# Decoder layer with a mixture of experts: expert tiles begun from the lists of five blocks, inside the cross-attention stage

## The chip, the cores and the metric

The kernel runs on one core of a Trainium2 chip. The metric is device time in microseconds (us), a median over runs. Engines are named as in the profile: PE is TensorE, DVE is VectorE, ACT is ScalarE, POOL is GpSimd, SP is SyncE.

## What is computed

The input is `x`, 4 sequences of 1024 tokens with 256 channels, and a context of 77 rows for each sequence. Three sublayers follow one another; after each one comes a residual and a layer norm:

```
x = layernorm(x + attn(x))         # gated delta rule: q, k, v projections, 4-tap causal convolution, silu, l2norm
x = layernorm(x + xattn(x, ctx))   # 16 heads of 64 over 77 context rows, masked softmax
x = layernorm(x + ffn(x))          # 8 experts, the top 2 of each token

probs = softmax(x @ router_w.T); keep the top 2, divide by their sum
g = x @ gate_w[e] + gate_b[e];  u = x @ up_w[e] + up_b[e]        # 256 -> 512
y = sum over the two experts of probs[e] * ((silu(g) * u) @ down_w[e] + down_b[e])
```

## The kernel before

Tokens are handled in 32 tiles of 128, and 4 tiles form a block, so there are 8 blocks. There are five stages, each with its own `Block` of five instruction streams, one per engine; a stage begins when all streams of the one before have ended. Every stream is written out by hand, runs in its written order, and waits on semaphores. There is no scheduler.

**`project_stage`** (line 100). For each block PE turns the normalised input (L335), makes eight column tiles of q, k, v (L379) and four gate tiles (L391). ACT copies each product out of PSUM twice (L463, L467), DVE adds three taps of the convolution to it (L617, three per column tile), PE turns the result back (L371) and ACT applies silu into `tok` (L456). POOL squares q and k (L299, two instructions of 128x1024 per block, in `squares`), DVE sums the squares (L603), and POOL makes the norms (L309 to L313) and scales `tok` by them (L316).

**`delta_stage`** (line 674). The recurrence. Near its end POOL fills `blank`, which SP stores over the DRAM tensor `list`: weight 0, and as destination one spare row of `y`.

**`cross_stage`** (line 1614). For each tile `g` of 32 a chain runs over all engines: PE scores, DVE scales them out of PSUM (`scaled_out`, L2189), POOL adds the mask (L1780), DVE takes the maximum and subtracts it (L2197, L2199), ACT takes exp (L2001), DVE sums and inverts (L2205, L2207), POOL scales (L1786), PE turns the weights and multiplies by V and the output projection (`attended`, L1885). After block `n` comes its norm (`x2t`, L1792, L1794, L2233, L2021), the store to the DRAM tensor `x2` (L1721), and the routing, one or two blocks late: `x2_turned` (L1899), `logits` (L1909), softmax and `top_two` on DVE, `counts` (L1916, L1917), and `entries` (L2130 to L2146), which gives each pair of token and expert a place in its expert's region of `list`. POOL writes the entries with eight indirect DMAs for each block (`listed_rows`, L1771). Behind the last block, DVE's `tile_list` (L2151 to L2166) turns the counts into two rows of 71 numbers: for each expert tile its expert (`tile_e`) and its place in the list (`tile_r`). SP also loads the experts' weights in this stage: gate and up early, down and the biases after block 6 (L2306 to L2314), into memory that the cross stage has used until then.

**`expert_stage`** (line 2318). 71 tiles of 128 entries (64 full ones and 7 for remainders), each of one expert. For tile `j`: SP loads its entries (L2361), DVE casts the two row numbers (L2497), POOL gathers 128 rows of `x2` (L2371), PE turns them (L2404), ACT copies (L2459), PE makes gate and up (L2415), DVE adds the biases (L2505 twice), ACT takes silu (L2464), DVE multiplies (L2512), PE turns (L2425), ACT copies (L2470), PE multiplies by the down weights (L2436), DVE adds the bias (L2519) and then weight and residual (L2523; the residual row is kept by ACT, L2477). POOL scatters the 128 rows to `y` (L2380), the token's first expert into the lower half of `y`, the second into the upper half. The next scatter waits until the one before has landed. PE's order is: gate and up of `j`, turn of the rows of `j+1`, turn of hidden `j-1`, down of `j-2`.

```
for j in range(FT + 2):
    if j < FT:
        known[j] = expert(pe, j)
        gate_up(j, known[j])
    if j + 1 < FT:
        x_turned(j + 1)
    if 1 <= j <= FT:
        h_turned(j - 1)
    if j >= 2:
        down(j - 2, known.pop(j - 2))
```

**`final_stage`** (line 2543). SP loads both halves of `y` block by block (16 DMAs of 512 KB, L2570, four blocks in flight), DVE adds the halves (L2608) and takes the moments (L2611, L2614), ACT the deviation (L2592), DVE inverts it (L2601, L2603), ACT normalises (L2584, four per block) and issues the store (L2588).

## Time and profile before

| | |
|---|---|
| median of 3 runs | 1759.49 us (1757.08 to 1759.88) |
| the profiled execution | 1761.76 us, span 1760.0 us |
| busy: PE, DVE, ACT, POOL | 1522.7, 1123.7, 735.7, 664.8 us |
| mean granted TensorE clock | 0.933 |
| DMA | 177.17 MB, mean 101 GB/s |

The span is the time from the first to the last instruction of the profiled execution. Busy time is a union: a PE row "x4" with 1.88 us is four matmuls that are issued one after the other and overlap, so its length is not four times the mean of one. In a timeline row the bracket tells how long the engine stood idle before it, and on whom it waited. POOL's DMA rows are the time in which it makes the descriptors; the transfer comes after. Clock 1.00 is full speed (2.4 GHz), 0.50 is half (1.2 GHz).

### The profile page before, as it was taken

How to read it: one execution, taken by the hardware profiler on the slowest of the kernel's cores; microseconds unless marked ns; L12 is line 12 of the kernel's file. 1: busy time of each engine (PE TensorE's matmuls, PEld its weight loads, DVE VectorE, ACT ScalarE, POOL GpSimd, SP SyncE). 2: the span in 40 equal slices, each digit the busy share in tenths (PEclk: the TensorE clock that was granted, in tenths of full speed). 3: DMA queues.
4: the chain of work that ended last, by engine and by line, in shares of the span. 5: the costliest groups of instructions: out<-in, count | busy, mean ns of one | idle time of the engine just before them, and what ended most of it. 6: DMA issues, size and time to landing. Idle time of an engine off the chain costs nothing. (4 is left out here: it accounts for less than half of the span.)

```text
span 1760.0 us, 30667 instructions
## 1 busy us (share of the span) xinstructions
PE 1522.7 (87%) x10698; PEld 1080.1 (61%) x10698; DVE 1123.7 (64%) x2342; ACT 735.7 (42%) x1625; POOL 664.8 (38%) x539
## 2 busy tenths in 40 slices
PE   6999954799999999957999999997379999999970
PEld 3555523788888887624777677776246666666640
DVE  5999985577777864522558787777434555555445
ACT  4667641234434444624455554542023333333324
POOL 1475646212333311011436555656423333333320
PEclk9999975799999999969999999998589999999995
DMA  3233337645556543261023230006011111111118
GB/s 103 85 132 119 148 134 191 165 119 163 149 156 151 137 123 137 85 208 56 6 79 128 85 126 28 13 25 224 29 28 49 46 46 46 47 49 43 49 34 286
DMA packets 180126, 177.17 MB, mean 101 GB/s; under 512 B 79640, under 2 KB 138700, under 8 KB 179852
## 3 DMA queue, kind: packets, MB, share of 16 engines
q1 hardware_dynamic: 163963, 145.23, 27.1%
q0 software_dynamic: 10400, 22.95, 3.9%
q10 hardware_dynamic: 5616, 7.08, 1.2%
q8 instruction: 87, 1.43, 0.3%
q14 instruction: 60, 0.48, 0.1%
HBM read 115.39 MB, written 59.81 MB: 100 GB/s over the span
## 5 line engine op out<-in xcount | busy, mean ns | idle before, releaser
L617 DVE SCALAR_TENSOR_TENSOR conv_y<-conv_in,taps,conv_y 128x512 f32<-128x512 f32 x192 | 185.1, 977 | 11.7 <-ACT conv_y L467 7.0
L2380 POOL DMA_INDIRECT y<-o,idx x71 | 83.5, 1176 | 241.6 <-DVE o L2523 233.8
L2459 ACT ACTIVATE xsT<-pX 128x256 f32<-128x256 f32 x71 | 27.3, 384 | 303.4 <-PE pX L2404 303.4
L2415 PE MATMUL pG<-w_gu,xsT 128*128 x284 | 135.5, 600 | 1.2 <-issue 0.6
L1831 PE MATMUL xQ<-late,last 128*128 128x512 f32 x256 | 128.4, 625 | 8.9 <-ACT late L1987 4.8
L2415 PE MATMUL pU<-w_gu,xsT 128*128 x284 | 134.3, 595 | 0.0
L2436 PE MATMUL pD<-late,hT 128*128 x568 | 134.2, 379 | 0.0
L379 PE MATMUL ps_j<-xnT,w_qkv 128*128 128x512 f32 x256 | 122.6, 603 | 0.0
L1786 POOL TENSOR_TENSOR sc<-sc,den 128x1232 f32<-128x1232 f32 x32 | 72.0, 2251 | 109.2 <-DVE den L2207 109.0
L2436 PEld LDWEIGHTS pD<-late,hT 128*128 128x128 f32 x568 | 102.5, 190 | 11.0
L2519 DVE TENSOR_TENSOR o<-pD,late 128x256 f32<-128x256 f32 x71 | 30.2, 425 | 121.4 <-PE pD L2436 121.4
L991 POOL DMA_DIRECT2D x<-x1t x32 | 18.3, 572 | 223.2 <-ACT x1t L1337 223.2
L1780 POOL TENSOR_TENSOR sc<-sc,madd 128x1232 f32<-128x1232 f32 x32 | 82.7, 2585 | 37.6 <-DVE sc L2189 37.6
L2415 PEld LDWEIGHTS pU<-w_gu,xsT 128*128 128x128 f32 x284 | 54.4, 192 | 69.0 <-issue 69.0
L1771 POOL DMA_INDIRECT list<-ent,idx x64 | 76.5, 1196 | 43.0 <-DVE ent L2146 26.8
L2505 DVE TENSOR_TENSOR u<-pU,last 128x512 f32<-128x512 f32 x71 | 49.1, 692 | 67.0 <-issue 50.1
L2371 POOL DMA_INDIRECT xs<-x,idx x71 | 68.5, 965 | 44.8 <-DVE idx L2497 24.7
L1831 PEld LDWEIGHTS xQ<-late,last 128*128 128x128 f32 x256 | 46.1, 196 | 53.6 <-issue 32.3
L2415 PEld LDWEIGHTS pG<-w_gu,xsT 128*128 128x128 f32 x284 | 54.2, 192 | 40.1 <-issue 36.6
L1885 PE MATMUL xO<-vw,aT 128*128 128x256 f32 (+1 forms) x320 | 76.5, 396 | 2.1 <-DVE x2t L2217 1.1
L2205 DVE TENSOR_REDUCE den<-sc 128x16 f32<-128x1232 f32 x32 | 46.0, 1436 | 49.2 <-ACT sc L2001 49.2
L1885 PE MATMUL xO<-last,aT 128*128 128x256 f32 (+1 forms) x320 | 72.0, 380 | 0.0
(339 smaller groups left out, 3614.3 us busy)
## 6 DMA issues: line engine op xcount, KB each, us to landing
carried<-qkvg SPq DMA_DIRECT2D x64, 256.0 KB, 5.3
qkvg<-tok SPq DMA_DIRECT2D x4, 2048.0 KB, 6.7
qkvg<-gate SPq DMA_DIRECT2D x8, 1024.0 KB, 9.5
qks<-qkvg SPq DMA_DIRECT2D x32, 256.0 KB, 4.7
y<-y SPq DMA_DIRECT2D x16, 512.0 KB
steps<-step SPq DMA_DIRECT2D x30, 256.0 KB, 4.3
qkvg<-carried SPq DMA_DIRECT2D x3, 2048.0 KB, 6.5
vw<-even SPq DMA_DIRECT2D x4, 1232.0 KB
```

Source lines behind the costliest of these rows:

```text
L379: mm = pe.matmul(ps_j[j % 2][:], w_qkv[:, c, j * P:(j + 1) * P], xnT[b][:, c, :], start=c == 0, stop=c == KD - 1)
L617: y = nc.vector.scalar_tensor_tensor(conv_y[m % 4][:], conv_in[b][:, m, k:k + BT], taps[:, m, k:k + 1], conv_y[m % 4][:], ALU.mult, ALU.add)
L1771: nc.gpsimd.indirect_dma_start(out=s["list"], out_offset=bass.IndirectOffsetOnAxis(ap=idx[:, k, t:t + 1], axis=0), in_=ent[:, t, k, :], in ...
L1780: nc.gpsimd.tensor_tensor(v, v, madd[b % 2][:].unsqueeze(1).broadcast_to([P, XH, CTX]), ALU.add).then_inc(masked, 1)
L1786: nc.gpsimd.tensor_tensor(v, v, over_keys(den[g % 2][:]), ALU.mult).then_inc(scaled, 1)
L1831: mm = pe.matmul(Q[:], w_q[:, c, j * P:(j + 1) * P], x1T[:, c, :], start=c == 0, stop=c == KD - 1)
L1885: mm = pe.matmul(O[:, (g % 2) * D:(g % 2 + 1) * D], aT[g % 2][0:rows(c), c, :], vw[b % 2][0:rows(c), c, :], start=c == 0, stop=c == KCH - 1)
L2371: nc.gpsimd.indirect_dma_start(out=xs[q][:], out_offset=None, in_=s["x2"].rearrange("t p d -> (t p) d"), in_offset=bass.IndirectOffsetOnAx ...
L2380: nc.gpsimd.indirect_dma_start(out=s["y"].rearrange("t p d -> (t p) d"), out_offset=bass.IndirectOffsetOnAxis(ap=idx[j % 8][:, 0:1], axis= ...
L2415: mm = pe.matmul(to[:], xsT[q][:, c, :], w_gu[:, bass.ds(e, 1), c, k * FF:(k + 1) * FF], start=c == 0, stop=c == KD - 1)
L2436: mm = pe.matmul(pD[q][:, 0:D], hT[q][:, k, :], w_d[:, bass.ds(e, 1), k, :], start=k == 0, stop=k == FK - 1)
L2505: nc.vector.tensor_tensor(to[:], frm[:], b_gu[:, bass.ds(e, 1), k * FF:(k + 1) * FF], ALU.add).then_inc(done, 1)
```

## The change

Four parts, each in the diff below, cut to its core.

1. In `project_stage` ACT squares q and k in place of POOL: the function `square(k)`, called for column steps 6 and 7.
2. The result `y` is added up in DRAM. `store_x2` stores each block of `x2` to `y` too, the scatter has `compute_op=ALU.add`, both experts of a token go to the same row, and the padding rows of `list` get spare rows of their own. The kept residual and its ACT copy go; DVE's last step is a multiplication by the weight. `final_stage` loads one 512 KB piece per block and adds nothing.
3. `expert_stage` is gone as a stage. Its five streams are functions called at the end of the cross stage's streams, with its buffers (`kT_0`, `vw_1`, `sc`, `aT`) and PSUM banks; `pD` has one bank where it had two. The tile list is made in two parts. `head_list` runs on DVE in block 6 behind tiles 1, 2 and 3 and lists HEAD = 32 full tiles from the counts of blocks 0 to 4. `rest_list` lists the other 39. Both are the former `tile_list` in pieces: `tiles_counted` is its first three instructions (L2151 to L2154), `tiles_begun` its scan, comparison and sum (L2155 to L2158), `tiles_placed` the next four (L2159 to L2162).
4. What ended the cross stage is put between the tiles by `between(j)`: DVE's norm terms, `entries(6)`, logits, `top_two(7)`, `entries(7)`, `rest_list`; POOL's deviations and the 16 list writes; PE's turns, logits and counts; ACT's norm, copies and exp; SP's last store.

```diff
+HEAD_BLOCKS = BLOCKS - 3
+HEAD = (HEAD_BLOCKS * BLK * P * 2 - NE * (P - 1)) // P
...
-                        nc.gpsimd.tensor_tensor(sq[:, :, k * DK:(k + 1) * DK], part, part, ALU.mult
-                                                ).then_inc(sq_done, 1)
...
+                    def square(k):
+                        act.wait_ge(tok_taken[0], n * (NCT // 2) + k + 1)
+                        act.wait_ge(tok_taken[1], n * (NCT // 2) + k + 1)
+                        act.wait_ge(ss_done, n)
+                        nc.scalar.activation(sq[:, :, k * DK:(k + 1) * DK], tok[b][:, :, k * DK:(k + 1) * DK],
+                                             ACT.Square).then_inc(sq_done, 1)
...
+                        if j in (6, 7):
+                            square(j - 6)
...
                 sp.dma_start(x2_v[n], x2t[:]).then_inc(x2_out, 16)
+                sp.dma_start(y_v[n], x2t[:]).then_inc(x2_out, 16)
...
         @block.gpsimd
...
+            def between(j):
+                if j == 0:
+                    x2_deviations(BLOCKS - 1)
+                if 2 <= j < 2 + BLK:
+                    listed_rows(BLOCKS - 2, (j - 2,))
+                if 9 <= j < 9 + BLK:
+                    listed_rows(BLOCKS - 1, (j - 9,))
...
         @block.tensor
...
+            def between(j):
+                if j in (1, 2):
+                    x2_turned(BLOCKS - 1, j - 1)
+                if j == 3:
+                    logits(BLOCKS - 1, X).then_inc(lg_done, 1)
+                if j == 6:
+                    pe.wait_ge(lg_sb, BLOCKS)
+                    counts(BLOCKS - 1, X).then_inc(cn_done, 1)
...
         @block.scalar
...
+            def between(j):
+                if j == 0:
+                    x2_norm(BLOCKS - 1)
+                if j in (1, 2):
+                    x2_out_of_psum(BLOCKS - 1, j - 1)
+                if j == 4:
+                    weights_exp(BLOCKS - 1)
...
         @block.vector
...
+            def head_list(part):
+                if part == 0:
+                    tiles_counted(ALU.is_ge)
+                    link(V.tensor_scalar(full[:], nt[:], -1.0, None, ALU.add))
+                if part == 1:
+                    tiles_begun(HEAD, full)
+                    link(V.tensor_tensor(ahead[:], full[:], ct[:], ALU.subtract))
+                    link(V.tensor_scalar(ahead[:], ahead[:], float(HEAD), 0.0, ALU.add, ALU.max))
+                    link(V.tensor_tensor(ahead[:], ahead[:], full[:], ALU.min))
+                if part == 2:
+                    tiles_placed(HEAD, full)
+                    V.tensor_copy(s["tile_r"][:, 0:HEAD], skip[:, 0:HEAD]).then_inc(listed, 1)
+                    V.tensor_copy(s["tile_e"][:, 0:HEAD], off[:, 0:HEAD]).then_inc(listed, 1)
+                    dve.wait_ge(listed, 2)
...
+                    if t and n == HEAD_BLOCKS + 1:
+                        head_list(t - 1)
+
+            def between(j):
+                if j == 0:
+                    norm_terms(BLOCKS - 1)
+                    dve.wait_ge(cn_done, 1)
+                    counts_out(BLOCKS - 2, X)
+                if j == 1:
+                    entries(BLOCKS - 2)
+                if j == 4:
+                    dve.wait_ge(lg_done, 2)
+                    logits_out(BLOCKS - 1, X)
+                    shifted_logits(BLOCKS - 1)
+                if j == 5:
+                    top_two(BLOCKS - 1)
+                if j == 7:
+                    dve.wait_ge(cn_done, 2)
+                    counts_out(BLOCKS - 1, X)
+                    entries(BLOCKS - 1)
+                if j == 8:
+                    rest_list()
...
+def expert_sync(nc, sp, x, s, between):
+    sp.wait_ge(x.listed, 2)
+    sp.wait_ge(x.list_out, 16 * HEAD_BLOCKS * BLK * 2)
...
+    def scatter(j):
+        q = j % 4
+        if j == 0:
+            pool.wait_ge(x.x2_out, 32 * BLOCKS)
+        pool.wait_ge(x.o_done, j + 1)
+        if j:
+            pool.wait_ge(x.o_out[(j - 1) % 4], 16 * ((j - 1) // 4) + 16)
+        nc.gpsimd.indirect_dma_start(
+            out=s["y"].rearrange("t p d -> (t p) d"),
+            out_offset=bass.IndirectOffsetOnAxis(ap=x.idx[j % 8][:, 0:1], axis=0),
+            in_=x.o[q], in_offset=None, compute_op=ALU.add).then_inc(x.o_out[q], 16)
...
-                dve.wait_ge(y_in[n], 32)
-                nc.vector.tensor_tensor(z[n][:], y[n % 4][:, 0], y[n % 4][:, 1], ALU.add).then_inc(z_sum, 1)
+                dve.wait_ge(y_in[n], 16)
```

Where the order moves, first ACT in the project stage, column steps 6 and 7 of one block (`tok` holds q, k, v after silu, `xnT` the next block's turned input). Before:

```order
L463 ACTIVATE conv_in<-ps_j 128x512
L467 ACTIVATE conv_y<-ps_j,taps 128x512
L456 ACTIVATE tok<-ps_t 128x4x128
L428 ACTIVATE xnT<-ps_x,ln_wb 128x512 x2
L463 ACTIVATE conv_in<-ps_j 128x512
L467 ACTIVATE conv_y<-ps_j,taps 128x512
L456 ACTIVATE tok<-ps_t 128x4x128
L479 ACTIVATE gate<-ps_g 128x512
```

The same place now:

```order
L466 ACTIVATE conv_in<-ps_j 128x512
L470 ACTIVATE conv_y<-ps_j,taps 128x512
L452 ACTIVATE tok<-ps_t 128x4x128
L460 ACTIVATE sq<-tok 128x4x256
L424 ACTIVATE xnT<-ps_x,ln_wb 128x512 x2
L466 ACTIVATE conv_in<-ps_j 128x512
L470 ACTIVATE conv_y<-ps_j,taps 128x512
L452 ACTIVATE tok<-ps_t 128x4x128
L460 ACTIVATE sq<-tok 128x4x256
L484 ACTIVATE gate<-ps_g 128x512
```

Two squares came in, one ahead of the copies of the next block's turned input, and no table load with them.

Second, PE behind the last tile of the cross stage (`xO` is the attention's output, `xX` the bank of the routing). Before:

```order
L1885 MATMUL xO<-vw_1,aT 128x256 x10
L1916 MATMUL xX<-pick,con 128x32
L1917 MATMUL xX<-pick,con 128x32
L1899 MATMUL xX<-con,x2t 128x128 x8
L1909 MATMUL xX<-w_r,x2T 128x8 x8
L1916 MATMUL xX<-pick,con 128x32
L1917 MATMUL xX<-pick,con 128x32
L1616 UNCONDITIONAL_BRANCH
L2395 UNCONDITIONAL_BRANCH
L2404 MATMUL pX<-con,xs_0 128x128 x2
```

The same place now (`kT_0` and `aT` hold expert rows, `xS`, `xT` and `xQ` are their banks):

```order
L1921 MATMUL xO<-vw_1,aT 128x256 x10
L1952 MATMUL xX<-pick,con 128x32
L1953 MATMUL xX<-pick,con 128x32
L2508 MATMUL xT<-con,kT_0 128x128 x2
...
L2519 MATMUL xT<-w_gu,aT 128x512
L2508 MATMUL xT<-con,kT_0 128x128 x2
L2529 MATMUL xQ<-con,sc 128x128 x4
L1935 MATMUL xX<-con,x2t 128x128 x4
```

The first expert tile's rows are turned directly behind the counts of block 6; the turns of `x2t` of block 7 come behind expert tile 1.

Third, DVE at the same place now:

```order
L2169 TENSOR_TENSOR wt<-wt,row 128x32
L2599 CAST idx_0<-rows_0 128x2
L2599 CAST idx_1<-rows_1 128x2
L2599 CAST idx_2<-rows_2 128x2
L2296 TENSOR_TENSOR x2t<-xr,xO 128x512
L2300 BN_STATS stats<-x2t 128x6 x2
L2307 BN_AGGR mv<-stats 128x2 x4
```

The three casts, which the first gathers wait for, stand ahead of the residual of block 7; before, they stood behind the whole tile list.

## Rows read from the trace of the kernel before

**Rows 1.** Busy time by window: PE, PEld, DVE, ACT, POOL, clock, DMA share, GB/s.
```profile
160.00:200.00 40.00, 38.31 (x144) 20.29 (x143) 38.97 (x50) 27.95 (x52) 18.12 (x10) 1.00 0.39 136
...
1235.00:1240.00 5.00, 5.00 (x18) 4.13 (x16) 1.69 (x8) 0.00 (x0) 0.00 (x0) 0.67 0.00 0
...
1720.00:1725.00 5.00, 0.00 (x0) 0.00 (x0) 2.39 (x5) 0.00 (x0) 0.00 (x0) 0.50 1.09 385
```

**Rows 2.** Groups by line (count | busy, mean ns | idle before, releaser): PE's turn of the convolution's result.
```profile
L371 PE MATMUL ps_t<-con,conv_y 128*128 128x128 f32 x256 | 39.8, 279 | 15.7 <-DVE conv_y L617 15.7
```

**Rows 3.** Timeline of PE, project stage: start, us, engine, line, [idle before <-releaser].
```profile
183.43 0.66 PE L371 MATMUL ps_t<-con,conv_y 128*128 128x128 f32 x4 [1.69 <-DVE conv_y L617]
...
244.21 1.11 PE L371 MATMUL ps_t<-con,conv_y 128*128 128x128 f32 x4 [5.90 <-DVE conv_y L617]
```

**Rows 4.** Timeline, DVE then POOL, same stage; last, L617's durations by source line.
```profile
91.77 13.34 DVE L617 SCALAR_TENSOR_TENSOR conv_y<-conv_in,taps,conv_y 128x512 f32<-128x512 f32 x9
...
98.80 4.19 POOL L299 TENSOR_TENSOR sq<-tok 128x1024 f32<-128x1024 f32 x2
...
L617 DVE SCALAR_TENSOR_TENSOR conv_y<-conv_in,taps,conv_y x192: 717/752/3992, 24.4 to 253.2; 128x512 f32<-128x512 f32 x192
```

**Rows 5.** Timeline of DVE, end of the project stage.
```profile
238.45 1.80 DVE L574 TENSOR_SCALAR sm<-sm 128x128 f32<-128x128 f32 x1
240.28 3.87 DVE L617 SCALAR_TENSOR_TENSOR conv_y<-conv_in,taps,conv_y 128x512 f32<-128x512 f32 x3
```

**Rows 6.** Groups by line: the cross stage's widest ScalarE function.
```profile
L2001 ACT ACTIVATE sc<-sc 128x1232 f32<-128x1232 f32 x31 | 38.1, 1228 | 53.0 <-DVE sc L2199 53.0
```

**Rows 7.** Timeline of DVE, cross stage: block 6, then the tile list.
```profile
1153.28 3.12 DVE L2132 TENSOR_TENSOR cum<-cum,cnt 128x8 f32<-128x8 f32 x4
...
1181.62 1.44 DVE L2197 TENSOR_REDUCE mx<-sc 128x16 f32<-128x1232 f32 x1 [2.52 <-POOL sc L1780]
...
1261.91 0.17 DVE L2151 TENSOR_TENSOR ct<-cum,con 128x8 f32<-128x8 f32 x1
...
1267.55 0.26 DVE L2166 CAST tile_e<-off 128x71 int32<-128x71 f32 x1
```

**Rows 8.** Timeline of PE, end of the cross stage and first expert tile.
```profile
1234.60 5.46 PE L1885 MATMUL xO<-vw,aT 128*128 128x256 f32 x16
...
1249.46 3.58 PE L1909 MATMUL xX<-w_r,x2T 128*128 128x8 f32 x16 [0.69 <-ACT x2T L2027]
...
1286.52 0.66 PE L2404 MATMUL pX<-con,xs 128*128 128x128 f32 x2 [28.10 <-DMA xs<-x,idx]
1287.75 3.78 PE L2415 MATMUL pG<-w_gu,xsT 128*128 x4 [0.56 <-issue]
```

**Rows 9.** Timeline, the same place: DVE's routing of block 7; SyncE's first row loads.
```profile
1253.15 0.19 DVE L2094 COPY lg<-xX 128x32 f32<-128x32 f32 x1 [6.20 <-PE xX L1909]
...
1281.51 8.49 SPq L2361 DMA_DIRECT2D rows<-list  x8
```

**Rows 10.** Timeline of PE, then DVE, two expert tiles in the steady part.
```profile
1502.97 1.88 PE L2415 MATMUL pG<-w_gu,xsT 128*128 x4
...
1508.79 1.88 PE L2415 MATMUL pG<-w_gu,xsT 128*128 x4
...
1509.12 0.42 DVE L2519 TENSOR_TENSOR o<-pD,late 128x256 f32<-128x256 f32 x1 [1.71 <-PE pD L2436]
```

**Rows 11.** Timeline of POOL: a scatter of the steady part, and the last one.
```profile
1510.41 1.19 POOL L2380 DMA_INDIRECT y<-o,idx  x1 [3.36 <-DVE o L2523]
...
1710.25 0.96 POOL L2380 DMA_INDIRECT y<-o,idx  x1 [2.90 <-DMA y<-o,idx]
```

**Rows 12.** Timeline of ACT, final stage; last, its deviation group by line.
```profile
1728.91 2.07 ACT L2584 ACTIVATE z<-z,shift,rstd 128x256 f32<-128x256 f32 x4
...
1755.85 0.38 ACTq L2588 DMA_DIRECT2D out<-z  x1
...
L2592 ACT ACTIVATE rstd<-mv,eps 128x4 f32<-128x4 f32 x8 | 2.4, 297 | 9.6 <-DVE mv L2614 9.6
```

524 lines of the change are left out of this document (254 added, 270 removed).

## The prediction

> **What bounds the kernel now.** I read the page first, then busy time by window, then the timelines at the borders of stages. The profiled execution took 1761.8 us (its span is 1760.0), the median is 1759.5, so I sum against 1761.8 and take off 2.3 at the end. Three places matter. In the project stage PE and DVE are both busy for 38 to 39 of 40 us, ACT for 28, at full clock [rows 1]. Between the cross stage's last attention and the first expert tile PE does nearly nothing. In the final stage the DMA engines are full at 385 GB/s [rows 1]. The expert tiles between are bound by PE, which has no gap there (part 3).
>
> **1. Squares from POOL to ACT.** PE waits for DVE's convolution 15.7 us in all [rows 2]. Of these 5.90 are at 244.2 [rows 3] and 2.2 behind it; the other 7.6 are five waits, one per block like that of 1.69 at 183.4 [rows 3]. DVE is late because of POOL: a tap takes 0.75 us in the median but up to 3.99 [rows 4], and the nine that begin at 91.8 take 13.3 us instead of 9 x 0.75 = 6.8, while POOL scales `tok` (about 4 us) and squares (4.19 for the two) [rows 4]. About half of the 6.5 lost is thus the squares', 3.3 per block. The squares' share is more than the wait, so without them DVE is ahead of PE, which waits no more: -7.6. At the stage's end DVE itself is the path: L574 takes 1.80 and three taps 3.87 instead of 2.26 beside the squares [rows 5], which gives -3.2. ACT pays 2 x 1024 elements; exp on 1232 takes 1.23 us [rows 6], so 1.02 each, 2.0 per block on an engine with 12 of 40 us free. The first stands ahead of the turned input's copies, which leaves PE about no slack there, so a few tenths per block may come back. I take **-11**, bounds -16 and 0.
>
> **2. `head_list`.** It costs less than the old list's 5.9 us (from 1261.9 to 1267.8) [rows 7], some 4.8 in three parts of 1.6. In block 6 DVE has a hole of 2.5 us before the maximum behind tile 2 [rows 7], a like one behind tile 1, none behind tile 3, where `top_two` already runs late. So +1.6 if each part ran at its own speed in these holes. But the holes are there because POOL is masking, and four additions of eight elements took 3.12 us there [rows 7] against 0.8 elsewhere. A `tensor_tensor` of the list that starts in a hole ends with POOL's instruction at the earliest, so parts 1 and 2 each push the maximum back by about 1.2. I take **+4**, bounds +1.6 and +8. The Trainium skill (SBUF — State Buffer, Who interferes with whom) says that a DVE instruction with two SBUF inputs contends with a GpSimd instruction that reads SBUF and blocks until it ends; by that rule the term is +4, without it +1.6, and the trace agrees with it.
>
> **3. The start of the experts.** Now the attention's last matmuls end at 1240.1, the logits of block 7 at 1253, and the first expert rows are turned at 1286.5, after 28.1 us of waiting [rows 8]. In between lie routing (DVE from 1253.15), the list, the last list writes, the border of the stage, and the row loads, issued only from 1281.5 on [rows 9]. After the change SP issues the row loads behind the expert weights (from about 1219), and the DMA engines are idle by 1235 [rows 1], so they have landed. DVE casts behind `top_two(6)` at 1237, POOL gathers, and by the 2.6 to 3 us from gather to turn the rows are there at about 1240.5, with the attention's end. PE turns them at about 1241: -45.5. Back come on PE: the turns, logits and counts of block 7, which at half clock lasted 1.1, 1.1, 3.6 and 1.0 us and at full clock about half: +3.4. In the second tile PE waits for the norm of block 7, whose terms DVE makes only behind tile 0: +1. The rest lies beside PE's 5.82, the distance of two tiles in the steady part [rows 10]: DVE idles 1.71 before the down bias [rows 10] and 0.96 before up's; its inserts are `top_two` 4.2, `entries` 3.4 and `rest_list` about 5.1. A hidden tile is needed 1.7 us after it is ready, so one insert may last about 4.4 us: only `rest_list`, next to `entries`, exceeds it: +1.4. POOL's two list writes in an iteration (2.5) with gather and scatter (2.8) make 5.3 of 5.82. ACT's two table loads fit into its idle time. The first tile's gate at low clock took 3.78 instead of 1.88 [rows 8, 10]; I leave that as it was. Sum, rounded, **-39.5**; bounds -44 (nothing comes back, the clock stays up) and -25 (each of the first ten tiles loses 1.5).
>
> **4. Adding scatter.** POOL waits for `o` 3.36 us before each scatter [rows 11]; only at the end does it wait for the landing of the one before: 0.96 of issue and 2.90 of idle [rows 11], a loop of 3.86 us. Reading the old row lengthens it by an amount that no row shows. Below, nothing; above, a whole second transfer, a loop of 7.7. I take that issue and wake-up, over half of the loop, are not paid twice, so a loop of 4.5 to 5.2, under 5.82: **0**. Removing `kept` frees 0.5 us of ACT per tile and some of DVE: idle engines, nothing. The single `pD` bank is free long before PE's next down: 0. The second store of `x2` (4 MB in all) meets idle DMA engines: 0.
>
> **5. Final stage.** 8 MB of loads become 4, and the sum on DVE goes. Then ACT is the bound: 2.07 us for four normalisations, 0.30 for the deviation, 0.38 to issue the store [rows 12] make 2.8 per block. Begin at 1717.5, first half megabyte at about 1721, DVE 1.8, table load and deviation 1.6, terms: first normalisation at 1725.2 (now 1728.9 [rows 12]), last at 1744.8, its store issued at 1746.9 instead of 1755.85 [rows 12]: **-9**, bounds -12 (the loads come sooner) and -4.
>
> **Sum:** -11 + 4 - 39.5 + 0 - 9 = -55.5, so 1706.3 as profiled, 1704 as median.
>
> **The rivals.**
> - *The scatter becomes the bound, slower than before.* Place: POOL waits for the landing before each of 71 scatters. It decides from a loop of 5.82 us on; from 5.82 + 55.5/71 = 6.6 on the gain is used up. Speaking for it: a read and a write of 128 scattered rows in sequence; at the upper bound's middle, 7.2 us, it costs 71 x 1.4 = +98: 1802. Against: the data part of 3.86 is small. 8%.
> - *The same, milder:* a loop of 5.9 to 6.6, on average +27: 1731. 8%. The Trainium skill (Collectives: The Full Stack, The bandwidth ceiling: the fold count and why AG ≠ RS ≠ AR) says that an add in the DMA path needs two source reads, two read descriptors per chunk, where a copy needs one. No row here shows such an add; taken for the whole loop the rule would give 7.7 and the first rival, taken for the data alone it leaves my 0.
> - *The inserts stall the pipeline.* DVE, ACT and POOL each wait inside `between` for PE and for one another, and what is queued behind them is the next tile. If each of the first ten tiles loses 2.5 us: +25 less the 2.4 counted: 1727. For: every stream is in order. Against: DVE's idle time per tile. 12%.
> - *The squares bring nothing,* since ACT's 1.0 us stands ahead of the copies for PE: 1715. For: PE and ACT meet there without slack. 9%.
> - *The early start isn't one:* the casts or gathers come late (weights landing late, rows queued behind them), 15 us lost: 1719. 3%.
>
> **How the numbers follow.** The forecast has 60%. Its own range is 1692 to 1715. To 8 in 10 belong the cases of squares, late gathers and inserts, which end at about 1727, and the lower part of the mild scatter: 1690 to 1734. Left out are the slow scatter and some of each tail. About 0.2%, 3.5 us, is what a measurement of this kernel can tell from no change. Slower: 8% and a little of the unnamed, 0.09; same 0.01; faster 0.90.
>
> **What would show it.** PE without waits for the convolution, its 15.7 us down to about 5; nine taps at about 10 us where they took 13.3. The first expert turn within 2 us of the last attention, and from then 71 tiles at 5.82, the first ten at about 6.3 on average. POOL waiting for `o` and not for the scatter before; were it the other way, part 4 is wrong and the sum with it. The last store issued 29 us after the final stage's start, where it was 38.

## The result and the profile after

| | before | after |
|---|---|---|
| median of all runs, us | 1759.1 (1757.1 to 1759.9) | 1720.1 (1716.7 to 1722.4) |
| profiled execution, us (its span) | 1761.8 (1760.0) | 1718.2 (1716.4) |
| PE, DVE, ACT, POOL busy in the span, us | 1522.7, 1123.7, 735.7, 664.8 | 1523.2, 1087.5, 724.6, 677.0 |
| end of the project stage (last gate turn on PE), us | 257.4 | 244.7 |
| first expert turn, last down product (starts), us | 1286.5, 1706.3 | 1238.5, 1671.1 |
| start of the final stage, last store issued, us | 1717.5, 1755.9 | 1683.1, 1711.9 |

The ratio is 0.9766, with a 95% interval from 0.9742 to 0.9791: 41 us less by the ratio, 39 by the medians, and 43.6 between the two profiled spans. A second comparison further down gave 0.9734 (0.9709 to 0.9760), 46 us by the medians. The forecast was 55.5, so 10 to 16 us of it didn't come.

**The project stage.** Groups by line of the kernel after, the turns of the convolution and its taps (count | busy, mean ns | idle before, releaser):

```profile
L367 PE MATMUL ps_t<-con,conv_y 128*128 128x128 f32 x256 | 39.6, 278 | 6.0 <-DVE conv_y L622 4.2 <-ACT carried L452 1.8
L622 DVE SCALAR_TENSOR_TENSOR conv_y<-conv_in,taps,conv_y 128x512 f32<-128x512 f32 x192 | 161.4, 850 | 24.2 <-ACT conv_y L470 19.5
```

PE's idle time before the turns is 6.0 us where it was 15.7 [rows 2]. A tap takes 0.85 us on average; before, the same 192 took 0.98. Timeline of DVE, the same stretch as [rows 4]:

```profile
89.50 10.01 DVE L622 SCALAR_TENSOR_TENSOR conv_y<-conv_in,taps,conv_y 128x512 f32<-128x512 f32 x9
```

The nine taps that took 13.34 us take 10.01. What is left above 6.8 stands beside POOL's scaling of `tok`.

**`head_list`.** Timeline of DVE, block 6, then POOL at the same time:

```profile
1158.27 3.89 DVE L2214 TENSOR_TENSOR ct<-cum,con 128x8 f32<-128x8 f32 x1
1173.53 0.16 DVE L2201 TENSOR_TENSOR_SCAN ct<-con,full 128x8 f32<-128x8 f32 x1
1173.73 2.69 DVE L2202 TENSOR_TENSOR of<-con,ct 128x256 f32<-128x256 f32 x1
...
1191.63 0.42 DVE L2208 TENSOR_TENSOR of<-of,full 128x256 f32<-128x256 f32 x1
```

POOL:

```profile
1159.52 2.60 POOL L1809 TENSOR_TENSOR sc<-sc,madd 128x1232 f32<-128x1232 f32 x1
...
1173.52 2.61 POOL L1809 TENSOR_TENSOR sc<-sc,madd 128x1232 f32<-128x1232 f32 x1
```

The subtraction of eight numbers takes 3.89 us and ends at 1162.16, POOL's masking at 1162.12. The comparison of 256 takes 2.69 and ends at 1176.42, the masking at 1176.13. With POOL idle, a `TENSOR_TENSOR` of 256 takes 0.42 (last line of DVE). Parts 1 and 2 each wait for POOL as the forecast had it. The scan at 1173.53, which also has two inputs in SBUF, takes 0.16 although the masking starts at 1173.52 by the profile; starts on POOL are rough, so the trace doesn't tell why this one got through. DVE's work falls back against the kernel before by 2.1 us at part 1, 1.4 at part 2 and 1.6 at part 3.

**The first expert tiles.** Timeline of PE:

```profile
1230.38 4.59 PE L1921 MATMUL xO<-vw,aT 128*128 128x256 f32 x20 [0.52 <-ACT aT L2057]
...
1238.50 0.66 PE L2508 MATMUL xT<-con,kT 128*128 128x128 f32 x2 [3.17 <-DMA kT<-x,idx]
1239.72 6.10 PE L2519 MATMUL xS<-w_gu,kT 128*128 x8 [0.56 <-ACT kT L2566]
...
1251.43 0.66 PE L1935 MATMUL xX<-con,x2t 128*128 128x128 f32 x4 [0.48 <-ACT x2t L2063]
...
1308.13 0.66 PE L2529 MATMUL xQ<-con,sc 128*128 128x128 f32 x4 [1.30 <-DVE sc L2613]
...
1316.50 0.69 PE L2508 MATMUL xT<-con,kT 128*128 128x128 f32 x2 [2.56 <-DMA kT<-x,idx]
1316.98 1.06 PE L2529 MATMUL xQ<-con,sc 128*128 128x128 f32 x4
1317.84 2.81 PE L2540 MATMUL xO<-late,aT 128*128 x8
```

The row `xQ L2529` is the turn of a tile's hidden rows, `xO L2540` its down product. The first turn comes at 1238.5 where it came at 1286.5 [rows 8], behind 3.2 us of waiting for the gather. PE's waits in the tiles are 0.48 for block 7's norm, 1.30 for `rest_list`, and 0.48, 0.44, 2.56 and 0.46 for gathers, 3.9 in all. Behind the 2.56 the clock is down: the hidden turn takes 1.06 us instead of 0.60, the down product 2.81 instead of 1.89. From the 16th tile on each takes 5.82 us, as before, measured from first gate product to first gate product. Why the gather is late stands on POOL, timeline from the late scatter on:

```profile
1307.75 1.81 POOL L2476 DMA_INDIRECT y<-vw,idx  x1 [4.98 <-DVE vw L2622]
1309.86 0.98 POOL L1800 DMA_INDIRECT list<-ent,idx  x1 [0.31 <-issue]
1311.14 0.96 POOL L1800 DMA_INDIRECT list<-ent,idx  x1 [0.30 <-issue]
1312.41 0.99 POOL L2465 DMA_INDIRECT kT<-x,idx  x1 [0.30 <-DVE idx L2599]
1313.70 1.62 POOL L2476 DMA_INDIRECT y<-vw,idx  x1 [0.30 <-issue]
```

`rest_list` holds DVE from 1299.9 to 1304.9, so the scatter starts late; two list writes stand behind it, and the gather behind these, 1312.41, lands for PE at 1316.50. Its landing is slow too: 4.05 us from issue to landing, and 3.4 to 4.6 for all eight gathers that stand behind two list writes, where the other 63 take 2.8 in the median and 4.0 at most. A scatter takes POOL 1.77 us on average, where it took 1.18 before. With two list writes an iteration is 0.98 + 1.80 + 2 x 0.97 and four gaps of 0.30: 5.9 us of a tile's 5.82. The sum alone doesn't make the gather late: in seven of the eight iterations with list writes POOL still waits 0.4 to 5.5 us for DVE's `vw` ahead of the scatter. What counts is that the gather stands last in the iteration, and starts 4.7 us behind a scatter whose start DVE sets.

**The end.** Timeline of POOL, then of ACT:

```profile
1671.16 1.55 POOL L2476 DMA_INDIRECT y<-vw,idx  x1 [2.99 <-DMA y<-vw,idx]
1675.58 1.55 POOL L2476 DMA_INDIRECT y<-vw,idx  x1 [2.87 <-DMA y<-vw,idx]
```

```profile
1690.91 2.07 ACT L2682 ACTIVATE y<-y,shift,rstd 128x256 f32<-128x256 f32 x4
...
1711.88 0.38 ACTq L2686 DMA_DIRECT2D out<-y  x1
```

The loop of a scatter, its landing and the next is 1.55 + 2.87 = 4.42 us, 3.86 before [rows 11]. The two differ in more than the add: the padding rows, which the last tiles of each expert hold, all go to one spare row before and to spare rows of their own after. The last store is issued 28.8 us after the final stage's start, 38.3 before.

### The profile page after: what moved, and what is told of

Same layout as the page of the kernel before. It is cut to its first block and busy times, and to the rows that moved or that the text cites. A ratio compares the mean times of both kernels' runs of the same rounds, so it can differ in the third digit from the quotient of the medians.

```text
span 1716.4 us, 30448 instructions
## 1 busy us (share of the span) xinstructions
PE 1523.2 (89%) x10698; PEld 1079.5 (63%) x10698; DVE 1087.5 (63%) x2352; ACT 724.6 (42%) x1572; POOL 677.0 (39%) x530
## 3 DMA queue, kind: packets, MB, share of 16 engines
q0 software_dynamic: 17216, 22.95, 8.1%
## 5 line engine op out<-in xcount | busy, mean ns | idle before, releaser
L2476 POOL DMA_INDIRECT y<-vw,idx x71 | 125.5, 1768 | 190.7 <-DVE vw L2622 180.3
L622 DVE SCALAR_TENSOR_TENSOR conv_y<-conv_in,taps,conv_y 128x512 f32<-128x512 f32 x192 | 161.4, 850 | 24.2 <-ACT conv_y L470 19.5
L2540 PE MATMUL xO<-late,aT 128*128 x568 | 135.4, 381 | 0.8 <-DVE vw L2620 0.8
L2519 PE MATMUL xS<-w_gu,kT 128*128 x288 | 132.2, 602 | 0.8 <-ACT kT L2566 0.6
L2607 DVE TENSOR_TENSOR sc<-xS,last 128x512 f32<-128x512 f32 x107 | 73.7, 692 | 60.6 <-PE xS L2519 57.2
L2540 PEld LDWEIGHTS xO<-late,aT 128*128 128x128 f32 x568 | 103.1, 192 | 12.5 <-issue 1.2
L2620 DVE TENSOR_TENSOR vw<-xO,late 128x256 f32<-128x256 f32 x71 | 30.1, 424 | 121.4 <-PE xO L2540 121.4
L2519 PEld LDWEIGHTS xS<-w_gu,kT 128*128 128x128 f32 x288 | 55.4, 193 | 56.3 <-issue 54.6
L1921 PEld LDWEIGHTS xO<-vw,aT 128*128 128x128 f32 (+1 forms) x320 | 63.6, 202 | 15.8 <-issue 5.1
L375 PEld LDWEIGHTS ps_j<-xnT,w_qkv 128*128 128x128 f32 x256 | 45.8, 193 | 40.7 <-issue 40.7
```

What stands on the lines that cost most here:

```text
L375: mm = pe.matmul(ps_j[j % 2][:], w_qkv[:, c, j * P:(j + 1) * P], xnT[b][:, c, :], start=c == 0, stop=c == KD - 1)
L622: y = nc.vector.scalar_tensor_tensor(conv_y[m % 4][:], conv_in[b][:, m, k:k + BT], taps[:, m, k:k + 1], conv_y[m % 4][:], ALU.mult, ALU.add)
L1921: mm = pe.matmul(O[:, (g % 2) * D:(g % 2 + 1) * D], aT[g % 2][0:rows(c), c, :], vw[b % 2][0:rows(c), c, :], start=c == 0, stop=c == KCH - 1)
L2476: nc.gpsimd.indirect_dma_start(out=s["y"].rearrange("t p d -> (t p) d"), out_offset=bass.IndirectOffsetOnAxis(ap=x.idx[j % 8][:, 0:1], axi ...
L2519: mm = pe.matmul(to[:], x.xsT[q][:, c, :], w_gu[:, bass.ds(e, 1), c, k * FF:(k + 1) * FF], start=c == 0, stop=c == KD - 1)
L2540: mm = pe.matmul(x.pD[:, 0:D], x.hT[q][:, k, :], w_d[:, bass.ds(e, 1), k, :], start=k == 0, stop=k == FK - 1)
```

## The experiments

Each run has a profile beside its times, so most readings below are of the traces: "offset" is by how much the same DVE and ACT instructions start earlier (minus) than in the kernel before's first profile, and "tiles" is the time from the first to the last gate product on PE (410.2 us before, 422.1 after). The ratio is to the kernel before on the same chip.

| run | ratio (95%) | offset at 260 | at 800 | at 1225 | tiles |
|---|---|---|---|---|---|
| the change, first | 0.9766 (0.9742 to 0.9791) | -12.7 | -7.5 | -2.2 | 422.1 |
| the change, again | 0.9734 (0.9709 to 0.9760) | -13.2 | -8.4 | -3.4 | 420.9 |
| the kernel before, again | 0.9998 (0.9979 to 1.0017) | 0.8 | -1.8 | -1.8 | 410.2 |
| squares back on POOL | 0.9804 (0.9774 to 0.9835) | 0.8 | -6.1 | -0.9 | 421.4 |
| squares alone | 0.9928 (0.9899 to 0.9957) | -12.4 | -17.7 | -17.6 | 409.7 |
| scatter without the add | 0.9682 (0.9650 to 0.9713) | -12.4 | -14.5 | -9.3 | 418.1 |
| gather three ahead | 0.9698 (0.9666 to 0.9730) | -12.2 | -14.0 | -8.8 | 415.8 |
| `head_list` in the holes | 0.9705 (0.9683 to 0.9727) | -12.3 | -11.1 | -10.4 | 421.1 |
| casts first | 0.9707 (0.9683 to 0.9731) | -13.2 | -13.0 | -7.7 | 422.1 |
| list writes spread | 0.9748 (0.9726 to 0.9769) | -11.9 | -13.3 | -8.1 | 419.3 |
| four repairs | 0.9664 (0.9643 to 0.9684) | -13.3 | -16.1 | -15.4 | 412.9 |
| five repairs | 0.9641 (0.9617 to 0.9665) | -13.3 | -13.1 | -12.4 | 412.9 |
| six repairs | 0.9640 (0.9614 to 0.9667) | -13.1 | -12.3 | -11.4 | 411.6 |

The column at 800 is a warning: ten of these programs, all that keep the squares on ACT and the second part of the change, are the same up to there, and stand between -7.5 and -16.1. The delta stage alone makes single executions differ by several microseconds. A difference of 5 us between two spans says nothing of the change; the same stretch in several traces does. The ratios have the same limit. Those of the four, five and six repairs lie clear of both intervals of the change; that of every single repair, and of the scatter without the add, touches the interval of at least one of the two comparisons, so what each of these edits brings is read from its trace.

### Squares back on POOL

```diff
+                    for k in range(2):
+                        pool.wait_ge(tok_taken[0], n * (NCT // 2) + k + 1)
+                        pool.wait_ge(tok_taken[1], n * (NCT // 2) + k + 1)
+                        pool.wait_ge(ss_done, n)
+                        part = tok[b][:, :, k * DK:(k + 1) * DK]
+                        nc.gpsimd.tensor_tensor(sq[:, :, k * DK:(k + 1) * DK], part, part, ALU.mult
+                                                ).then_inc(sq_done, 1)
...
-                        if j in (6, 7):
-                            square(j - 6)
```

> The changed kernel with the squares back on POOL. My theory: the project stage's gain is real (PE's end-of-stage turns moved from 257.4 to 244.7 us, -12.7) and it is passed on in full, since every later stage begins when the one before ends; the 5 us by which the offset between the two traces shrinks in the delta stage (from -12.7 to -7.5) are PE clock dips of single executions (granted clock 0.91 to 0.92 in three stretches of 20 us where the kernel before shows 1.00). Then this kernel takes 12 us more than the changed one, about 1732, and its trace has PE's wait for the convolution at about 15.7 us again. Rival: the delta stage gives a part back whatever the clock, by transfers that it waits for; then only 7 to 8 us more, about 1727.5. Second rival: the squares brought nothing, 1720.

Measured 1725.2 us median, ratio 0.9804: 6.7 us more than the change by the first comparison, 12.3 by the second. In the trace the old state is back, as groups by line of this kernel show:

```profile
L374 PE MATMUL ps_t<-con,conv_y 128*128 128x128 f32 x256 | 40.3, 281 | 15.8 <-DVE conv_y L620 15.8
L620 DVE SCALAR_TENSOR_TENSOR conv_y<-conv_in,taps,conv_y 128x512 f32<-128x512 f32 x192 | 185.2, 977 | 12.8 <-ACT conv_y L470 8.0
```

PE waits 15.8 us again, and the project stage ends where it ended before the change. The second rival (nothing) falls by this trace and by the next run; by the times alone it wouldn't, since this run's interval overlaps that of the change's first comparison. How much is passed on this run alone doesn't tell.

### Squares alone

The kernel before, and of the change only `square(k)` on ACT.

> The kernel before with nothing changed but the squares, now on ACT. Passed on in full: 1759.1 - 12 = about 1747. With a part given back in the delta stage: about 1751.5. Nothing: 1759. Together with the run with the squares back on POOL it tells whether the gain depends on the rest of the change: it should not.

Measured 1746.7, ratio 0.9928: 12.7 us less, with an interval from 7.6 to 17.8. PE's wait is 6.0 us, as after the change. The gain is the squares' alone and doesn't need the rest. The interval holds the full 12 us and, at its edge, the 7.6 of a part given back, so it hardly decides between them.

### The kernel before, and the change, once more

> The kernel before itself, for a second profile. Theory: its first profiled execution (1761.8 us) was about 3 us slower than usual in the delta stage and behind it; this one is 0 to 6 us ahead of it at 800 us. Then the squares' 12.4 us are passed on nearly whole. Rival: the same as the first within 1 us; then 3 to 5 us of the squares' gain are really given back behind the project stage.

> The changed kernel itself once more, beside the two repaired ones and the kernel before, for a second profile and a comparison on one chip. Up to the cross stage it is the same program as five kernels already profiled, whose offsets against the one execution of the kernel before differ by up to 6 us behind the delta stage (-7.5 to -14.5). Theory: noise of single executions; here -7 to -15 again, and 1716 to 1722 in time.

The second profile of the kernel before is 1.8 us ahead of the first at 800 us. With it there are three traces with the squares on POOL (0, -1.8, -6.1: on average -2.6 at 800 us, and +0.5 at 260) and eleven with the squares on ACT (on average -12.8 at 800, -12.7 at 260). So of 13.3 us at the project stage's end 10.2 arrive at the cross stage, on average, with a scatter of some 3 us in either group. Whether the other 3 are lost to a cause or to these few traces stays open. So it isn't shown that the 5 us of the first pair's shrinking (-12.7 to -7.5) were chance, as I had it: 3 of them remain on average. The change's second median is 1716.2.

### Scatter without the add

```diff
-            in_=x.o[q], in_offset=None, compute_op=ALU.add).then_inc(x.o_out[q], 16)
+            in_=x.o[q], in_offset=None).then_inc(x.o_out[q], 16)
```

> The changed kernel with a scatter that writes and doesn't add: the sum of the two experts and the residual is left out of the output. It tells what the adding costs. The trace shows POOL's instruction for the scatter at 1.77 us on average where the plain one took 1.19, and in the iterations with two list writes POOL has 0.98 + 1.80 + 2 x 0.97 and four gaps of 0.30, 5.9 us of work for a tile of 5.82: gathers come late (PE waits 0.5 to 2.6 us for them five times, 4.4 us in all). My theory: the adding costs nothing in the steady part (tiles at 5.82 either way) and 0.6 us per iteration in the first fourteen, so this kernel gains 1 to 4 us: 1716 to 1719. My forecast's 'nothing' would be 1720. Rival: the add lengthens the landing that POOL waits for and the steady part hides a part of it, more than 6 us gained: under 1714.

Measured 1702.8, ratio 0.9682: 14.8 us under the change by the first comparison, 9.1 by the second, more than I had expected of it. The trace has 8.6 of it in two places. The tiles take 418.1 us instead of 422.1. And the end is shorter; timeline of POOL:

```profile
1656.86 0.97 POOL L2476 DMA_INDIRECT y<-vw,idx  x1 [5.54 <-issue]
1660.03 0.97 POOL L2476 DMA_INDIRECT y<-vw,idx  x1 [2.20 <-DMA y<-vw,idx]
1663.17 0.97 POOL L2476 DMA_INDIRECT y<-vw,idx  x1 [2.17 <-DMA y<-vw,idx]
```

The loop is 0.97 + 2.17 = 3.14 us instead of 4.42, and from the last down product to the final stage's start it is 7.4 us instead of 12.0. From issue to landing a scatter takes 2.6 us in the median instead of 4.0. In the steady part a tile takes 5.82 us with the add and without.

What the 4.0 us in the tiles are, PE's timeline tells at the place of the 2.56 us:

```profile
1308.53 0.44 PE L2508 MATMUL xT<-con,kT 128*128 128x128 f32 x2 [1.89 <-DMA kT<-x,idx]
...
1309.24 1.89 PE L2540 MATMUL xO<-late,aT 128*128 x8
```

This is the only wait for a gather over 0.2 us that is left in the tiles: those of 0.48, 0.44 and 0.46 are gone, 2.56 has become 1.89, and behind it the down product runs at full clock, 1.89 us. The two tiles around the longest wait take 7.33 and 7.92 us instead of 7.34 and 10.13. But 1.89 us remain without any add, and the gathers behind list writes still take 3.2 to 4.3 us to land: the list writes and the late scatter make a wait by themselves.

So the rival was right in size and wrong in place: the add costs nothing in the steady part, where 5.82 us cover it, 4.0 in the first tiles, and 4.6 at the end, where each scatter waits for the landing before it and nothing covers that.

### Gather three tiles ahead

```diff
-LIST_LEAD, ROW_LEAD = 3, 2
+LIST_LEAD, ROW_LEAD = 4, 3
```

> The changed kernel with the gather three tiles ahead instead of two, and the casts of the row numbers four ahead instead of three; nothing else. My theory: the missing microseconds of the early start are mostly gathers queued on POOL behind list writes and scatters (PE's waits of 0.48, 0.44, 2.56 and 0.46 us, and the fall of PE's clock behind the longest, 1.6 us more for that tile). With one more tile of lead they vanish: 1720.1 - 4 to 5.5 = about 1715.5. Rival 1: the waits come from the inserts on DVE (rest_list, 5.0 us), the gathers are late only because of these; then only about 1 us is gained, 1719. Rival 2: the gather itself is slow beside the adding scatter's traffic; then nothing changes.

Measured 1707.8, ratio 0.9698. Waits of PE from the cross stage's end to 1330 us, first two lines (total, times, longest):

```profile
PE xT L2508 <- DMA kT<-x,idx: 3.2, 1, 3.2
PE xQ L2529 <- DVE sc L2613: 1.3, 1, 1.3
```

The only wait for a gather left is the one ahead of the first tile. The 12th tile takes 5.82 us where it took 10.13, the clock doesn't fall there any more, and the tiles take 415.8 us: 6.3 less. My theory holds, rivals 1 and 2 fall: `rest_list`'s wait of 1.3 is still there without a late gather, and the gathers behind list writes still take up to 4.5 us to land, but PE no longer waits for them. What the ratio has beyond 6.3 us by the first comparison lies ahead of the experts (offset -14.0 at 800 us), in code that is the same.

### List writes spread

```diff
-                if 9 <= j < 9 + BLK:
-                    listed_rows(BLOCKS - 1, (j - 9,))
+                if j in (12, 15, 18, 21):
+                    listed_rows(BLOCKS - 1, ((j - 12) // 3,))
```

> The changed kernel with the list writes of block 7 in the tiles 12, 15, 18 and 21 instead of 9 to 12; the gather is still two tiles ahead. It tells whether it is these writes, queued on POOL ahead of the gathers, that make gathers late. Theory: PE's waits of 2.56 and 0.46 us and the slow clock behind the first (1.6 us) go, 0.48 and 0.44 at tiles 6 and 7 (block 6's writes) stay: about 4.5 us gained, 1715.5, and PE's distance of tiles falls from 8.62 to about 5.2 in the twelfth. Rival: the late scatter behind rest_list alone delays the gather: the 2.56 us stay and the run takes 1720.

Measured 1717.6, ratio 0.9748; the tiles take 419.3 us, 2.8 less, not 4.5. Timeline of PE, the turns with a wait behind `rest_list`:

```profile
1326.74 0.44 PE L2508 MATMUL xT<-con,aT 128*128 128x128 f32 x2 [0.51 <-DMA aT<-x,idx]
...
1345.50 0.44 PE L2508 MATMUL xT<-con,kT 128*128 128x128 f32 x2 [1.08 <-DMA kT<-x,idx]
...
1363.60 0.44 PE L2508 MATMUL xT<-con,kT 128*128 128x128 f32 x2 [0.43 <-DMA kT<-x,idx]
...
1381.53 0.44 PE L2508 MATMUL xT<-con,kT 128*128 128x128 f32 x2 [0.26 <-DMA kT<-x,idx]
```

The wait of 2.56 and the slow clock are gone though `rest_list` still delays its scatter, so the late scatter alone doesn't make that wait; it takes the list writes behind it. But each of the four moved pairs of list writes leaves a wait of 0.3 to 1.1 behind it. So it is not the crowding of four iterations: with a lead of two tiles a single iteration with two list writes is already too long, though POOL idles 2.7 us ahead of each of these scatters. The lead is the repair, not the spreading. The ratio itself tells no difference from the change; the tiles in the trace do.

### `head_list` in DVE's waits for ACT

```diff
+        HOLES = [(HEAD_BLOCKS + 1, 1), (HEAD_BLOCKS + 1, 2), (HEAD_BLOCKS + 1, 3), (HEAD_BLOCKS + 2, 1),
+                 (HEAD_BLOCKS + 2, 2)]
...
                     if g + 1 < TILE_N:
                         maximum(g + 1)
+                        if (n, t) in HOLES:
+                            head_list(HOLES.index((n, t)))
...
-                    if t and n == HEAD_BLOCKS + 1:
-                        head_list(t - 1)
```

(and `head_list`'s instructions in five parts instead of three)

> The changed kernel with head_list cut in five parts, each between the maximum and the sums of a tile (blocks 6 and 7), where DVE waits 1.3 us for ACT's exponential and POOL is idle, instead of three parts behind tiles 1 to 3 of block 6, where POOL masks. In four executions the old places cost 5.1 to 5.3 us between 1160 and 1225 us, and in them one addition of eight numbers took 3.89 us where such a one takes 0.17 elsewhere, ending with POOL's masking. Theory (blocked by POOL): in the new places each instruction takes its own 0.17 to 0.43 us and the parts, 0.3 to 1.3 us long, lie in the wait: offset against the kernel before unchanged across blocks 6 and 7, 5 us gained: 1715. Rival (DVE is simply full in these blocks, any 4.8 us of work there cost about their time): 1720, with the loss moved to the new places.

Measured 1709.1, ratio 0.9705. Timeline of DVE, the first part in its new place:

```profile
1150.24 0.16 DVE L2216 TENSOR_TENSOR ct<-cum,con 128x8 f32<-128x8 f32 x1
1150.44 0.43 DVE L2217 TENSOR_TENSOR many<-ct,k 128x256 f32<-128x256 f32 x1
1150.90 0.42 DVE L2219 TENSOR_REDUCE nt<-many 128x8 f32<-128x256 f32 x1
1151.35 0.17 DVE L2224 TENSOR_SCALAR full<-nt 128x8 f32<-128x8 f32 x1
1151.67 1.44 DVE L2288 TENSOR_REDUCE den<-sc 128x16 f32<-128x1232 f32 x1 [0.15 <-ACT sc L2045]
```

The subtraction takes 0.16 us instead of 3.89, the whole part lies in the wait, and from 1160 to 1225 us the offset changes by 0.7 instead of 5.3: the theory holds. At the end of the last attention 3.2 us of these 4.6 are left: its 20 products take 6.27 us here, 4.59 after the change (see the clock below).

### Casts first

```diff
+                    if t == 3 and n == BLOCKS - 1:
+                        for j in range(LIST_LEAD):
+                            dve.wait_ge(x.rows_in[j], 16)
+                            V.tensor_copy(x.idx[j][:], x.rows[j][:, 1:3]).then_inc(x.idx_done, 1)
                     if t == 3 and n:
                         top_two(n - 1)
...
-    for j in range(LIST_LEAD):
-        indices(j)
```

> The changed kernel with the first three casts of row numbers ahead of top_two of block 6 (DVE waits 1.56 us there for ACT) instead of behind it. The gather then starts about 5 us sooner and PE's first expert turn follows the attention's end without the 3.2 us of waiting for the gather. Theory: 3 us gained at the turn, and if PE's half clock in the first gate (6.1 us for eight matmuls where later ones take 3.60) comes from that wait, up to 2.5 more: 1714.5 to 1717. Rival 1: the clock had fallen before (0.83 to 0.85 in the last blocks), the gate stays at 6.1 us: 1717. Rival 2: the next thing is late (norm of block 7, weights): nothing, 1720.

Measured 1713.4, ratio 0.9707, but not by this: PE's first turn comes 3.9 us behind the attention's last product, 3.5 before the edit, and the tiles take the same 422.1. Rival 2 happened, with two things late that I hadn't named. PE's longest wait there, by its waits:

```profile
PE xX L1952 <- DVE pick L2163: 3.3, 1, 3.3
```

and the casts themselves, in DVE's timeline:

```profile
1229.91 0.56 DVE L2351 CAST idx<-rows 128x2 int32<-128x2 f32 x3 [5.75 <-DMA rows<-list]
```

The second makes the first. The rows landed only at 1229.9, behind the transfers of the weights and biases; DVE waited 5.75 us for them, with `top_two` queued behind the casts; and block 6's counts on PE, which need `top_two` and stand ahead of the turn, waited in their turn. After the change, with the casts behind `top_two`, PE didn't wait for the pick. The better ratio is that of a program whose upstream part ran well (-13.0 at 800 us); the edit has no share in it that a trace shows.

### Four, five and six repairs

The four: the lead, the holes, the casts first, and `rest_list` in two parts. The fifth moves the counts, the sixth is the row loads (and, for them, the last two parts of `head_list` one tile earlier):

```diff
 # four: rest_list
-                if j == 8:
-                    rest_list()
+                if j in (9, 10):
+                    rest_list(j - 9)
 # five: PE
-            pe.wait_ge(lg_sb, BLOCKS - 1)
-            counts(BLOCKS - 2, X).then_inc(cn_done, 1)
...
             def between(j):
+                if j == 0:
+                    pe.wait_ge(lg_sb, BLOCKS - 1)
+                    counts(BLOCKS - 2, X).then_inc(cn_done, 1)
 # six: SP, and only these two casts ahead of top_two
                     load_experts_late(sp, a, s)
+                    expert_rows(sp, x, s, range(ROWS_FIRST))
                     sp.wait_ge(sc_done, 3 * TILE_N)
                     load_experts_last(sp, a, s)
```

> The changed kernel with four repairs together: gathers three tiles ahead, head_list in DVE's waits for ACT, first casts ahead of top_two, and rest_list in two parts (tiles 9 and 10) instead of one at tile 8. If they add up: 6.4 (measured by the trace of the run with the lead) + 5.2 + 3 + 1.3 = 16 us under the changed kernel, 1704, or 1701 if the first gate's clock comes back. If one wait hides another: 1707 to 1710.

> The four repairs, and the counts of block 6 on PE behind the first expert tile's gate instead of ahead of its turn. The run with the casts first gained nothing at the turn, since PE, which works in order, then waited 3.3 us for top_two's pick (2.9 with the four repairs) in these counts, ahead of the turn. Theory: that wait goes, the turn moves up by about 2.5 us, to where the gather lands: 2 to 3 us under the run with four repairs, about 1699.5. Rival: the first gather is late anyway, since the row loads land behind the weights' transfers (the casts waited for them to 1229.9 us): under 1 us gained.

> As the kernel with five repairs, and the first two row loads on SP ahead of the biases' load (4 MB) instead of behind it, head_list's last parts one tile earlier for that, and only these two casts ahead of top_two. Theory: rows land in time, the first gather is done with the attention's end, PE turns within 1 us of it, its clock stays up in the first gate (3.6 us instead of 5 to 6.4): 3 to 5 us under the kernel with five, about 1696. Rival: the clock is already down through the last blocks (granted 0.83 to 0.85) and the gate takes 5 us or more: about 1698. If the later biases hold up the first bias addition, nothing is gained.

Medians 1702.0, 1698.3 and 1697.1, ratios 0.9664, 0.9641 and 0.9640. All three are faster than the change beyond both of its intervals; the last is 17 to 22 us faster by the ratios. Between four and five, and between five and six, the times tell no difference (their intervals overlap), the traces do. Timeline of PE, six repairs, end of the attention and first tile:

```profile
1226.71 0.38 PE L2531 MATMUL xT<-con,kT 128*128 128x128 f32 x2
1227.66 3.69 PE L2542 MATMUL xS<-w_gu,kT 128*128 x8 [0.56 <-ACT kT L2589]
1231.19 0.38 PE L2531 MATMUL xT<-con,kT 128*128 128x128 f32 x2
1231.41 0.31 PE L1955 MATMUL xX<-pick,con 128*128 128x32 f32 x2
```

The first turn follows the last attention product at once (3.4 us with four repairs, 3.6 with five, 3.5 after the change), and the first gate takes 3.69 us instead of 6.10. With four repairs PE waited 2.9 us for the pick; with five it waited 3.6 for the gather instead, as the rival had it: the casts waited for the rows to 1225.9. So the fifth repair by itself brought nothing at the turn. The sixth did, and it may not need the fifth: timeline of DVE, six repairs:

```profile
1223.75 0.18 DVE L2167 TENSOR_SCALAR pick<-pick 128x32 f32<-128x32 f32 x1
```

The pick is ready 2.9 us before the attention's last product ends, so the counts wouldn't have waited in their old place. No run has the early row loads with the counts there. `rest_list` in two parts costs no wait any more: the 11th and 12th tile take 5.82 us each, where they took 7.34 and 10.13 after the change and 7.32 and 5.82 with the lead alone.

## Why the prediction was right or wrong

The time (1720, in the range of 1690 to 1734) and the sign were right, the size was not: 39 to 46 us of 55.5. Term by term, of the two first profiles:

| term | forecast | measured |
|---|---|---|
| 1 squares | -11 | -12.7 at the stage's end, -7.5 at 800 us in this pair, -10.2 on average |
| 2 `head_list` | +4 | +5.3 |
| 3 first turn | -45.5 | -45.8 (-48.0, of which -2.2 is the offset at 1225) |
| 3 work moved into the tiles | +6 | +12.8 |
| 4 scatter | 0 | +0.8, between last down and final stage |
| 5 final stage | -9 | -9.2 |
| sum | -55.5 | -43.6 |

1. **Squares.** Right in mechanism and size: waits for the convolution from 15.7 to 6.0 us (I had said about 5), nine taps at 10.0 (about 10). The rival that they bring nothing is out. Of the 6.0 DVE makes 4.2, at the end of the stage; the other 1.8 are one wait for ACT at 225 us, where I had kept back a few tenths per block. How much of it reaches the cross stage is known only as an average: 10.2 of 13.3, with a scatter of some 3.
2. **`head_list`.** The mechanism was right: instructions of parts 1 and 2 ended with POOL's masking. Here the Trainium skill was the better guide than the holes: its page SBUF — State Buffer, Who interferes with whom, says that a DVE instruction with two SBUF inputs contends with GpSimd's reads. The trace agrees: 3.89 us for eight numbers beside the masking, 0.16 in the run that puts it where POOL is idle. The price was 5.3, not 4: part 1 cost 2.1 and part 2 1.4, where I had taken 1.2 beyond the hole for each, and part 3 cost its own 1.6; the last 0.2 come behind it.
3. **The first turn** came where I put it, and that is partly luck, since two things that the forecast didn't see cancelled: the attention's end, 1240.1 before, came 2.9 us sooner beside the offset of 2.2, and the turn stayed bound to DVE's casts behind `top_two` and to the gather. So PE turned 3.5 us behind the attention instead of 1, and with this the first gate stayed slow.
4. **The tiles** are where the forecast failed, by 7 us. The step is "POOL's two list writes in an iteration (2.5) with gather and scatter (2.8) make 5.3 of 5.82", from which I took that gathers aren't late. It was wrong twice. The 2.8 are a plain scatter's: the adding one holds POOL 1.8 us instead of 1.2, which makes 5.9. And the sum isn't the test: what decides is whether the gather, last in its iteration, lands in time with a lead of two tiles. It isn't so even with a plain scatter, when `rest_list` has made the scatter late (1.89 us of waiting in the run without the add, with list writes behind it), nor in a single iteration with list writes (0.3 to 1.1 in the run that spreads them). In sum late gathers cost 6.6 us by the tiles' lengths against the run with three tiles of lead: 3.9 are waits, 1.6 slow clock, the rest lies next to the waits. About 4.2 of the 6.6 go without the add. The other parts were near: 3.0 us for the turns, logits and counts (3.4), 0.5 for the norm (1), 1.3 for `rest_list` (1.4). Another 0.9 is at the end of the stage, where PE's down products wait for the single `pD` bank, which I had costed at 0 by the steady part. Some 0.5 us I can't place.
5. **The scatter's loop** was right: 4.42 us, under 5.82, the forecast's 4.5 to 5.2 a little high. Both rivals of a bound scatter are out: in 67 of 71 cases POOL waits for DVE, 180.3 of its 190.7 us. What I left out is that a price can be paid on the issuing engine and at the end of the stage; the run without the add puts 4.0 and 4.6 us there. The rule of the Trainium skill that I weighed (Collectives: The Full Stack, The bandwidth ceiling: the fold count and why AG ≠ RS ≠ AR), two source reads for an add, would have given 7.7 us, taken for the whole loop of 3.86. The trace shows 4.42. The fair comparison is the same kernel without the add, since its padding rows go to the same places: its loop is 3.14 us, twice that would be 6.3, and a scatter lands after 4.0 us instead of 2.6, half as much again and not double. Why the kernel before needs 3.86 for a plain one and not 3.14 no run tests; its padding rows share one spare row.
6. **Final stage.** Right: 28.8 us to the last store (29).

The rival "the inserts stall the pipeline" (1727, 12%) is nearest to what happened: its place was right, its size of 2.5 us per tile too large, and its mechanism, waits in `between`, only a part; the larger part was the queue behind them on POOL. That the time still fell inside the range owes to the range, which was wide enough for such a stall; the main forecast's own range ended at 1715.

## What to carry to other kernels

Before an engine that only issues DMAs is given more of them, start at the instruction that another engine paces (here the scatter) and add up, with the new durations and not those of the old form, everything from there to the landing of the transfer that the bound engine waits for. Compare this with the lead of that transfer; an iteration that just fits the loop's period isn't enough. If it is near, give one more iteration of lead. Small instructions belong where their own engine waits and POOL is idle as well: the same list making cost 5.3 us in one place and 0.7 in another. And an instruction moved ahead on an in-order engine takes its own wait along: the casts ahead of `top_two` brought nothing, since they waited for rows that landed late and held up `top_two` and what needs it. With the row loads (and the counts) moved as well the turn came 3.5 us sooner and the gate took 1.4 to 2.6 us less.
